# Reordered work lists in a two-layer attention and mixture-of-experts kernel: openings, last units, one load and its wait, a third bank

## The reference

```
x = x + cross_attention0(layernorm(x), ctx)        # 16 heads of 16
x = x + moe(layernorm(x))                          # 8 experts of 352, two per row, and a shared expert of 704
x = x + cross_attention1(layernorm(x), ctx)        # the same with biases
x = x + gated_low_rank(layernorm(x))               # y = x + sum_e gate[b,e] * (x A_e^T) B_e^T, rank 64
```

## Time and profile before

| | |
|---|---|
| runs of before | 487.47, 488.12, 488.65 us (median 488.12) |
| the profiled execution | 488.73 us, span 487.0 us |
| PE busy | 465.0 us, 95% of the span |
| DVE, POOL, ACT busy | 289.7, 240.8, 201.2 us |
| chain that ended last | PE 77%, DVE 7%, ACT 6%, DMA 4%, issue 3% |
| mean granted TensorE clock | 0.993 |
| DMA | 52.98 MB, mean 109 GB/s |

### The profile page before, as it was taken

The page is one execution under the profiler, slowest core; times in us unless marked ns, Lnnn a source line. Parts: engine busy times, 40 slices in busy tenths (PEclk is TensorE's granted clock), DMA queues, the critical chain, the costliest instruction groups (busy, mean ns, idle before and its releaser), DMA issues.

```text
span 487.0 us, 9539 instructions
## 1 busy us (share of the span) xinstructions
PE 465.0 (95%) x3156; PEld 383.3 (79%) x3156; DVE 289.7 (59%) x652; ACT 201.2 (41%) x451; POOL 240.8 (49%) x321
## 2 busy tenths in 40 slices
PE   7899999998999999998999999999998899999897
PEld 6677767685777788777999999999997666767677
DVE  5769986543353122326455454554455788998986
ACT  3455775466620022002332332323332455676841
POOL 6313443145336566209995552322332745768482
PEclk9999999999999999998999999999999899999999
DMA  8999400020002223999413332232115600000015
GB/s 275 404 395 351 69 12 1 1 87 2 0 1 88 84 93 109 334 318 331 84 45 98 100 108 68 69 87 66 45 44 150 208 2 1 1 1 1 15 31 172
DMA packets 48047, 52.98 MB, mean 109 GB/s; under 512 B 15329, under 2 KB 42274, under 8 KB 47746
## 3 DMA queue, kind: packets, MB, share of 16 engines
q1 hardware_dynamic: 34594, 23.02, 17.2%
q0 software_dynamic: 7616, 20.19, 12.4%
q10 hardware_dynamic: 5792, 9.18, 6.2%
HBM read 35.25 MB, written 17.12 MB: 108 GB/s over the span
## 4 chain that ended last, share of the span: by engine, by line
PE 77%; DVE 7%; ACT 6%; DMA 4%; issue 3%; POOL 1%; ACTq 1%; SPq 0%; POOLq 0%
PE banks L1232 10%; PE banks L1285 10%; PE banks L1336 6%; PE banks L346 5%; PE banks L1337 5%; PE banks L360 5%; PE banks L1340 5%; PE banks L324 5%; PE banks L313 5%; PE banks L1358 3%; PE banks L1362 3%; PE banks L1359 3%; PE banks L1348 3%; PE banks L1767 2%; ACT xn L125 2%
## 5 line engine op out<-in xcount | busy, mean ns | idle before, releaser
L115 POOL TENSOR_TENSOR rstd<-var,mhalf 128x2 f32<-128x2 f32 x30 | 20.8, 695 | 82.6 <-DVE var L108 82.6
L1162 ACT ACTIVATE hg<-banks 128x352 f32<-128x352 f32 x39 | 18.1, 464 | 98.5 <-PE banks L1340 93.8
L1509 DVE TENSOR_TENSOR hgT_lo<-banks,hgT_hi 128x256 fp32r<-128x256 f32 x78 | 24.1, 350 | 58.0 <-ACT hgT_hi L1169 58.0
L1336 PE MATMUL banks<-w_hi,xgT_hi 128*128 x156 | 55.4, 356 | 2.8 <-ACT xgT_hi L966 2.2
L507 DVE TENSOR_REDUCE mx<-banks 128x16 f32<-128x1024 f32 x32 | 39.1, 1221 | 22.5 <-PE banks L324 22.4
L1337 PE MATMUL banks<-wd,xgT_hi 128*128 x156 | 50.9, 328 | 0.0
L1285 PE MATMUL banks<-sdn,big 128*128 128x256 f32 x192 | 47.5, 393 | 0.0
L1285 PEld LDWEIGHTS banks<-sdn,big 128*128 128x128 f32 x192 | 34.1, 189 | 12.6 <-issue 9.0
L1063 POOL DMA_INDIRECT expert_rows_in<-xn,slot x32 | 31.4, 980 | 18.4 <-issue 7.3
L324 PE MATMUL banks<-kvb,qT 64*128 64x256 f32 x256 | 36.9, 407 | 1.2 <-ACT qT L428 0.6
L1340 PE MATMUL banks<-w_hi,xgT_lo 128*128 x156 | 37.9, 324 | 0.0
(11 more groups left out here) (250 smaller groups left out, 1164.2 us busy)
## 6 DMA issues: line engine op xcount, KB each, us to landing
w_hi<-in_egu POOLq DMA_DIRECT2D x2, 2816.0 KB, 21.6
expert_rows_in<-zeros SPq DMA_DIRECT2D x1, 5304.0 KB, 40.9
xn<-expert_rows_in SPq DMA_DIRECT2D x39, 128.0 KB, 2.0
y_all<-choices_out SPq DMA_DIRECT2D x16, 256.0 KB, 5.5
wd<-in_egu ACTq DMA_DIRECT2D x8, 352.0 KB, 9.7
wd<-in_egu ACTq DMA_DIRECT2D x4, 704.0 KB, 13.7
out_x<-x SPq DMA_DIRECT2D x7, 256.0 KB, 2.1
x<-in_x SPq DMA_DIRECT2D x2, 768.0 KB, 7.5
```

The source lines that it names most:

```text
L1336: nc.tensor.matmul(to, xgT_hi[:, c, k, :], hi, start=(k == 0), stop=False)
```

## The change

It has these parts. (1) Opening of the first attention: values wait for wq and wv alone (32 instead of 48); wo counts on `router_in`, for which `project_o(0)` waits on PE ("o0") and the router's split on DVE; unit 2's statistics stand ahead of the copy of values. (2) Last unit of both attentions: scores(7, 1) ahead of values(6). (3) First FFN: banks and ACT's buffers of the gates rotate over three from factor 12 on; `copy_turned` stands ahead of `normalise2`; `stats2(6)` ahead of the first split. (4) The loads for experts 6 and 7 go from ACT's queue to SP's, behind the fetch of block 6. (5) Opening of the second attention: 5 filler matmuls, normalising unit 1 ahead of the second query copy, unit 2's statistics behind the second shift. (6) The last step: logits ahead of values(5) in another bank, taken by ACT; the choice at step 12, gates at 14, factors weighed at 14, matrices ahead of the output projection of unit 6; the rows' work of units 3 to 7 stands later in all lists.

```diff
@@ attention, tensor @@
+            other_work("tensor", f"q{u}")          # in project_q, behind its wait
...
             if u == 0:
                 first_project_q(1)
+                other_work("tensor", "second queries")
...
-            if u >= 1:
+            other_work("tensor", f"v{u}")
+            if 1 <= u < NU - 1:
                 values(u - 1)
             other_work("tensor", 2 * u)
             scores(u, 1)
+            if u == NU - 1:
+                values(u - 1)
@@ attention, scalar @@
         first_copy_xT(1)
+        if combine is not None:
+            normalise(1)
         first_copy_q(1)
-        normalise(1)
+        if combine is None:
+            normalise(1)
@@ attention, vector @@
             if u == 0 and combine is None:
+                dve.wait_ge(*x_here[2])
+                stats(2)
                 kv.values(dve)
...
-            if u + 2 < NU and (u > 0 or combine is not None):
+            if 0 < u < NU - 2:
                 stats(u + 2)
             other_work("vector", 2 * u)
             shift(u, 1)
-            if u == 0 and combine is None:
-                dve.wait_ge(*x_here[2])
+            if u == 0 and combine is not None:
                 stats(2)
@@ load_ffn0, split_router, kv0 @@
-            sp.dma_start(wo[0][:, :, :], split(wo0)).then_inc(attn0_in, 16)
+            sp.dma_start(wo[0][:, :, :], split(wo0)).then_inc(router_in, 16)
-            nc.vector.wait_ge(router_in, 16)
+            nc.vector.wait_ge(router_in, 32)
-        kv0 = KeysValues(..., v_here=(attn0_in, 16 * 3))
+        kv0 = KeysValues(..., v_here=(attn0_in, 16 * 2))
+                       "o0": lambda: nc.tensor.wait_ge(router_in, 32)
@@ shared expert @@
+        def place(n):
+            return n % 2 if n < NH else n % 3
+        def gate_at(n):
+            return psum[(0, 1, 6)[place(n)]]
...
-            return (psum[n % 2], HIGH) if n % KS == KS - 1 else (psum[2 + n % 2], slice(0, P))
+            return (gate_at(n), HIGH) if n % KS == KS - 1 else (psum[(2, 3, 7)[place(n)]], slice(0, P))
...
-            wait(nc.tensor, silu_done, n - 1)
             if n < NH + 2:
+                wait(nc.tensor, silu_done, n - 1)
                 wait(nc.tensor, u_copied, n - 1)
+            elif n == NH + 2:
+                nc.tensor.wait_ge(routed, 1)
             else:
-                wait(nc.tensor, h2_done, n - 1 - NH)
+                wait(nc.tensor, silu_done, n - 2)
+                wait(nc.tensor, h2_done, n - 2 - NH)
@@ scalar_on @@
                 if n == 0:
                     normalise2(3)
+                if 3 <= n + 2 < NU:
+                    copy_turned(n + 2)
                 if n + 4 < NU:
                     normalise2(n + 4)
-                if 3 <= n + 2 < NU:
-                    copy_turned(n + 2)
...
             copy_rows(0)
-            act.wait_ge(d_ready, 16)
-            load_w(act, 6, E, w_in[5])
-            load_d(act, 6, E, 1, w_in[5])
@@ sync_on @@
-            for b in range(NX, NB):
+            for b in range(NX, NX + 3):
+                fetch(sp, b)
+            sp.wait_ge(d_ready, 16)
+            load_w(sp, 6, E, w_in[5])
+            load_d(sp, 6, E, 1, w_in[5])
+            for b in range(NX + 3, NB):
                 fetch(sp, b)
@@ vector_on @@
             stats2(5)
+            stats2(6)
             for u in range(3, NU):
                 split_transposed(u)
-                if u + 3 < NU:
-                    stats2(u + 3)
+                if u == 3:
+                    stats2(7)
@@ row_logits, take_logits @@
-            nc.tensor.wait_ge(o_copied, 5)
+            wait(nc.tensor, events1["xT_ready"], Q_STEPS)
...
-            v.tensor_copy(gt["p"][:, :, :], PSW[...]).then_inc(f_g, 1)
+            nc.scalar.activation(gt["p"][:, :, :], PSX[...], ACT.Copy).then_inc(f_g, 1)
```

More of the change, by code:

```diff
@@ L1229, in up @@
                 return
[L1230 removed]
+            for w, bank, done in ((0, gate_at(n), g_ready), (1, up_at(n)[0], u_ready)):
                 for a, (m, v, k) in enumerate(terms):
[L1232 removed]
+                    last = nc.tensor.matmul(bank[:, :], m[:, k, w * 6 * P + j * P:w * 6 * P + (j + 1) * P],
                                             v[g][:, k, :], start=(a == 0), stop=(a == len(terms) - 1))
@@ L1818, in load_ffn1 @@
             sp.dma_start(wr[:, :, :], split(wr_in)).then_inc(ffn1_in, 16)
-        tensor_work = {"keys and values": lambda: keep_warm(nc, psum[0], mem["ident"], 26), 9: lambda: turn3(0), 11: lambda: turn3(1), 12: row_logits,
-                       13: lambda: turn3(2), 14: lambda: turn3(3), 15: lambda: turn3(4),
-                       "last output but one": lambda: batch_matrix(0),
-                       16: lambda: (batch_matrix(1), product3(0), turn3(5), product3(2)),
-                       "end": lambda: (turn3(6), product3(1), product3(3), product3(4), turn3(7), product3(5), product3(6),
-                                       product3(7)),
-                       "x6": lambda: nc.tensor.wait_ge(f_xT, 1), "x7": lambda: nc.tensor.wait_ge(f_xT, 2),
-                       "o5": lambda: nc.tensor.wait_ge(f_g, 1)}
@@ L1835, in xattn_ffn_kernel @@
-        vector_work = {6: lambda: stats3(0), 8: lambda: stats3(1), 9: second_half_rows,
-                       10: lambda: stats3(2), 12: lambda: (stats3(3), stats3(4)), 13: take_logits, 14: choose,
-                       15: lambda: (gates(), split3(4), stats3(5)), "last output but one": lambda: (stats3(6), split_matrix(0)),
-                       16: lambda: (split_matrix(1), split3(5), add3(0)),
-                       "end": lambda: (stats3(7), add3(2), add3(1), split3(6), add3(3), add3(4), split3(7), add3(5), add3(6),
-                                       add_last())}
```

36 lines of the change are left out of this document (13 added, 23 removed).

## The result

The changed kernel took 490.72 us (median of six, 490.1 to 493.03), the kernel before, run beside it, 488.02: a ratio of 1.0062 with an interval of 1.0032 to 1.0092. It is slower by 2.7 us. The forecast was 487.1 in a range of 485.0 to 488.9, so both the number and the sign are wrong.

A forecast was written before the change was run, and what follows sets the result against it. PE has work nearly throughout, so each edit was priced by the PE wait it shortens or makes. Terms -2.1 - 1.8 - 0.4 + 0 + 0.2 + 2.3 + 0.8 = -1.0 gave a median of 487.1 us, range 485.0 to 488.9.

The forecast's parts named there:

- The opening and the FFN: First attention's opening and first FFN: shorter PE waits were to gain 2.1 and 1.8 us.
- First expert blocks: PE's wait ahead of block 1: low matmuls start at 222.5, gain 0.4 us, bounds 0 and 2.2.
- the dearer choice: Last step: by the skill's rule, rstd would also hold DVE, ending the choice 0.4 to 0.7 later; left out of the sum.
- SP's loads: 0: Loads of experts 6 and 7 on SP's queue: POOL's split is 20 us ahead of the need, so 0.
- rival C: Expert blocks: block 7's rows land late behind SP's loads, PE waits 4, 491 us; chance 0.1.
- Last unit, second opening, choice: First attention's last unit 0, second attention's opening 0, choice in the last step +0.2 us.
- The end: +2.3: Turn 6 waits 2.9 for DVE's split of unit 5 behind the adds; 2.3 us lost (2.0 to 2.6).
- The clock: +0.8: At the end, PE's clock falls to 1.2 GHz after the wait of 2.9, costing 0.8 us.
- Rival A: The end costs less, with no fall of the clock and the choice not held: 485.0 us; chance 0.25.
- rival B: Edits cancel: expert start gives nothing, clock costs 1.7, choice 0.4 more; 488.8 us at worst; chance 0.28.

The follow-up runs named there:

- loads_wait: after_held with ACT's loads of the experts' weights started only when all 32 scatters have landed; 495.86 us, ratio 1.0105.
- start_before: after_held with the kernel before's opening of the first attention and its shared FFN; 496.72 us, ratio 1.0129.
- after_held: The control: changed kernel with register moves on PE holding the loaded expert numbers at zero or above; 496.25 us, ratio 1.0110.
- before_d0: Kernel before with expert 0's down weights (high part) loaded by transfers of their own, plus the register moves of after_held; 492.89 us, ratio 1.0093.
- d0_first: after_held with the high part of expert 0's down weights loaded first by three transfers of their own; 490.32 us, ratio 0.9977.
- d0_loads_act: d0_first with the loads of experts 6 and 7 back on ACT; 491.54 us, ratio 1.0074.
- best: d0_first with the kernel before's end, register moves on four of ten loads only, and constant low-part waits from block 16; 480.74 us, ratio 0.9855.

## Why the prediction was wrong

**The opening and the FFN** were right as local terms: 1.74 for 2.1 and 1.9 for 1.8. In the opening wv landed at 12.4 rather than 11.9, which is as much as it came short.

**First expert blocks: this step failed.** It said "-0.4" and took for granted that the 3.9 us gained ahead of it pass through. It priced the place by what PE waited for in the kernel before, DVE's subtraction from 218.09 for 3.97. It reckoned the low matmuls from that unmoved time, 222.5, and yet added the 3.9 in full, as if all of this moved along. (That they started at 222.36 is luck: what bound them there was something else.) Whether that subtraction can start earlier depends on a transfer that released nobody in the trace: POOL's load of the high parts. Its time to landing stood in the trace before, in the view of the tile wd on POOL, and I didn't look for it; here from the kernel before, and behind it from the changed one (the longest is in both that of the third of the three transfers):

```profile
DMA to landing us min/median/max: 7.7/10.8/20.1
```

```profile
DMA to landing us min/median/max: 4.1/13.0/22.4
```

In the kernel before the third issue, some 1.84 behind the first at 195.19, plus 20.1 gives 217.1: 1.0 ahead of DVE's start at 218.09. In the changed kernel it is 198.46 + 22.4 = 220.8. So the transfer had 1.0 us of slack and came 3.7 us *later*, while its reader was ready 3.9 earlier. It is later because ACT's loads, which start 3.8 earlier, now overlap the last scatters: these land 5.9 behind the last issue instead of 2.5 (SP fetches the first rows at 196.34 and 194.46 then, the last scatters are issued at 190.45 and 192.00), POOL can issue only behind them, 1.4 later, and the landing takes 2.3 longer. The third transfer takes the longer, the more of ACT's loads are issued ahead of it:

| kernel | POOL's first issue behind ACT's first, us | issue to landing of the third transfer, us |
|---|---|---|
| loads_wait | 0.2 | 15.1 |
| start_before | 1.9 | 19.7 |
| before | 1.9 | 20.1 |
| changed | 7.1 | 22.4 |
| after_held | 7.9 | 22.3 |

start_before shows that the start's gain is lost whole, before_d0 that it wasn't this transfer in the kernel before, and d0_first that it is in the changed one. The bounds of the term, 0 and -2.2, could not hold this: with the gains ahead of it the term is +3.8.

That POOL's subtraction holds DVE's was right: 3.97 and 3.90 beside it, 1.02 without. The Trainium skill, "SBUF — State Buffer", section "Who interferes with whom", says that a VectorE instruction with two SBUF inputs contends with a GpSimd one that reads SBUF. The trace agrees in these rows, and in the two operations of the choice beside POOL's residual and low part, 1.02 and 1.20. Beside rstd, whose inputs lie in SBUF too, it does not: two operations with two inputs, at 447.97 and 448.18, took 0.17 and 0.18 while rstd ran from 447.65 for 0.71, and the other profiles with this choice show the same. So the dearer choice that the prediction drew from the rule, 0.4 to 0.7 more, did not come: it ended at 449.3, forecast 449.7.

**SP's loads: 0** was right for the changed kernel, and no block waited for its rows (rival C: block 7's rows were fetched at 228.7 and PE never stopped for them). That the move is worth 4 us once nothing else binds, only d0_loads_act shows.

**Last unit, second opening, choice** (0, 0, +0.2): -0.1, 0 and -0.1.

**The end: +2.3** was right, 2.3 by the order (turn 6 at 6.4 behind the last projection, forecast 6.55, its wait 2.81, forecast 2.9). **The clock: +0.8** was right in kind and undersized for the profile: one half-speed stretch costs 1.0 to 1.1 and there are two in a row there, 2.1 (12.2 against d0_first's 10.0). Other kernels with this end had one or none. The step assumed a single stretch of 3.4 as in the rows of before.

So in the profile: 0 from the start, -0.1 from the choice, +2.3 and +2.1 make 4.3, as measured; in the median, most likely with less of the clock, 2.7. Rival A is out, since the clock fell and the choice was held; rival B had the right direction, edits that cancel at the expert start, but put only 0.4 on it.

What stays open: how much of best's gain is the moves and how much the waits on registers; why the start is longer beside some runs of before; and how often the half-speed stretch of the end comes, which differs between executions of one kernel.

## What to carry to other kernels

Before a gain is carried past a join, list everything that the join needs, not only what came last in the trace: here a transfer with 1 us of slack stood behind a busy vector engine, came later instead of earlier, and took the whole 3.8 us. The test is to start the stage earlier on paper and to ask, for each wait in it, whether its source moves too; a transfer behind other large ones can move later, as this one did by 3.7 us. And where one large transfer serves several consumers, give the first consumer its own small one: three more issues took the ratio from the control's 1.0110 to 0.9977.

## What the runs showed of the hardware

- An earlier start of large loads made small scatters ahead of them land later: 5.9 us behind the last issue with overlap, 2.5 without (control and loads_wait). The third of three direct loads on POOL's queue, 480 KB, needed 22.4 us behind ACT's loads and 15.1 when it was issued together with them (changed kernel and loads_wait); expert 0's alone, 96 and 128 KB each, landed in 8.3 to 10.0 us in d0_first.
- A PE wait of 2.8 us was followed by a half-speed stretch of 6.8 us in two kernels, of 3.4 us in three and by none in one, all with the same end. Each 3.4 us cost 1.0 to 1.2 there, where PE is the chain.
- Two small DVE operations with two SBUF inputs took 0.17 and 0.18 us beside POOL's rstd (0.71 us); beside POOL's residual and low part (1.28 and 1.27 us) such operations took 1.02 and 1.20.
- Register moves that bound four loaded numbers cost about 0.25 us per load on PE, by one pair of profiles (2.5 us over ten loads, good to about 1), in a stretch in which it has no pause.
